# First phase of a two-layer decoder kernel: the cap of the decay inside the masked product, context by feature, cross scores of four strips at once, and a new order

## The reference, cut to what matters

```python
# state-space block: 32 heads of 16 channels, state 128
h = exp(A * dt_t)[...] * h + (dt_t * B_t) x_t ;  y_t = C_t . h          # scan over the 128 tokens
y = _rmsnorm(y + Dp * x_heads, norm_w) * silu(z) ;  x = x + y @ out_proj_w.T
# cross attention, 16 heads of 16 features, keys and values from ctx_1024
q = heads(layernorm(x) @ Wq.T + bq); k = heads(ctx @ Wk.T + bk); v = heads(ctx @ Wv.T + bv)
scores = q k / 4 - 10000 * (1 - mask) ; x = x + softmax(scores) @ v
# then the feed-forward of layer 0: shared expert + top 2 of 16 experts
```

## Time and profile before

| | before |
|---|---|
| median of 3 runs | 4044.49 us (4042.93 to 4050.74) |
| profiled execution, its own time | 4028.71 us |
| span in that profile | 4027.1 us |
| phase 1, 2, 3 (about, from the windows) | 0 to 1780, 1780 to 2080, 2080 to 4027 us |
| busy, whole span | PE 93%, PEld 73%, DVE 77%, ACT 69%, POOL 63% |
| mean granted TensorE clock | 0.973 of full speed |

### The profile page before, as it was taken

How to read it: one execution, slowest core, us unless ns; L and a number is a source line. 1 busy time by engine, 2 the same in 40 slices (tenths; PEclk the granted TensorE clock), 3 DMA queues, 4 the chain that set the end, 5 groups by cost and what they waited for, 6 DMA issues and landing times.

```text
span 4027.1 us, 119475 instructions
## 1 busy us (share of the span) xinstructions
PE 3741.4 (93%) x34582; PEld 2920.7 (73%) x34583; DVE 3082.5 (77%) x8792; ACT 2793.7 (69%) x8434; POOL 2523.8 (63%) x3252
## 2 busy tenths in 40 slices
PE   5999999999999999979978999999999999999997
PEld 4888888888888888867755666666666666666664
DVE  5888888888888888845546777777777777777775
ACT  4778777778888788844436666767667666766764
POOL 4566655656666566622236777777777777777774
PEclk8999999999999999979989999999999999999998
DMA  4334432333333333324420111111011111111110
GB/s 132 134 116 125 137 123 95 115 116 100 111 117 117 116 108 108 113 74 146 144 90 26 34 32 31 34 31 34 28 33 32 32 33 31 34 30 31 32 30 17
DMA packets 222650, 304.24 MB, mean 76 GB/s; under 512 B 57216, under 2 KB 176256, under 8 KB 222592
## 3 DMA queue, kind: packets, MB, share of 16 engines
q1 hardware_dynamic: 197632, 249.83, 19.5%
q0 software_dynamic: 19200, 52.45, 4.0%
q10 hardware_dynamic: 5760, 1.24, 0.2%
HBM read 239.18 MB, written 64.23 MB: 75 GB/s over the span
## 4 chain that ended last, share of the span: by engine, by line
PE 39%; issue 21%; DVE 16%; POOL 10%; ACT 9%; DVEq 2%; DMA 1%; ACTq 1%; POOLq 0%; SPq 0%
PE Q L1553 10%; PE Q L1546 8%; PE Q L1558 5%; PE Q L1933 3%; PE Q L1779 3%; PE Q L1587 3%; POOL arena L673 2%; DVE mx L1135 2%; PE Q L1791 2%; ACT arena L1348 2%; POOL arena L681 1%; ACT arena L1345 1%; PE Q L1874 1%; POOL arena L678 1%; ACT arena L1342 1%
## 5 line engine op out<-in xcount | busy, mean ns | idle before, releaser
L1558 PE MATMUL Q<-ident,arena 128*128 128x128 f32 x3488 | 587.5, 285 | 109.8 <-ACT arena L1282 34.3
L1558 PEld LDWEIGHTS Q<-ident,arena 128*128 128x128 f32 x3488 | 408.3, 143 | 350.0 <-issue 168.3
L1553 PE MATMUL Q<-Wkvl,arena 128*128 128x512 f32 x1024 | 520.8, 601 | 1.5 <-ACT arena L1497 0.8
L673 POOL TENSOR_TENSOR arena<-arena 128x1024 f32<-128x1024 f32 x256 | 481.6, 1902 | 37.0 <-DMA arena<-cum_rows 36.7
L744 POOL TENSOR_TENSOR l<-l,half_pow 128x8 f32<-128x8 f32 x192 | 317.5, 1654 | 146.0 <-DVE l L1154 145.9
L1466 ACT ACTIVATE arena<-Q,mx 128x128 f32<-128x128 f32 x1024 | 359.8, 386 | 6.2 <-DVE mx L1135 6.2
L1381 ACT ACTIVATE arena<-Q,mx 128x128 f32<-128x128 f32 x1024 | 287.2, 386 | 101.5 <-DVE mx L960 97.3
L1546 PE MATMUL Q<-arena,Win 128*128 128x128 f32 x2560 | 347.6, 280 | 1.3 <-DVE arena L890 1.3
L1587 PE MATMUL Q<-ident,arena 128*128 128x128 f32 x2048 | 322.9, 282 | 22.2 <-ACT arena L1381 12.1
L1546 PEld LDWEIGHTS Q<-arena,Win 128*128 128x128 f32 x2560 | 324.9, 196 | 6.3 <-DVE arena L890 2.0
L914 DVE TENSOR_TENSOR arena<-arena,Q 128x1024 f32<-128x1024 f32 x256 | 311.8, 1218 | 14.0 <-ACT arena L1336 7.0
(11 more groups left out here) (292 smaller groups left out, 10195.7 us busy)
## 6 DMA issues: line engine op xcount, KB each, us to landing
arena<-cum_rows SPq DMA_DIRECT2D x256, 512.0 KB, 6.3
arena<-routed_rows SPq DMA_DIRECT2D x144, 128.0 KB, 2.0
expert_rows<-arena POOLq DMA_DIRECT2D x144, 128.0 KB, 2.0
arena<-in_x_dram SPq DMA_DIRECT2D x128, 128.0 KB, 4.4
arena<-in_ctx_dram SPq DMA_DIRECT2D x128, 128.0 KB, 3.0
x_rows<-arena SPq DMA_DIRECT2D x128, 128.0 KB, 1.7
arena<-x_rows SPq DMA_DIRECT2D x128, 128.0 KB, 2.1
out_dram<-arena SPq DMA_DIRECT2D x64, 128.0 KB, 1.7
```

Source lines behind the costliest of these rows:

```text
L673: tell(g.tensor_tensor(E8[j], E8[j], cums[:, 8 * j:8 * j + 8].unsqueeze(2).broadcast_to([P, 8, T]), ALU.subtract), "diff")
L1553: last = mm(out, lhs(c), rhs(c), start=c == 0, stop=c == n - 1)
L1558: last = nc.tensor.transpose(out[:, c * P:(c + 1) * P], src[:, c * P:(c + 1) * P], ident[:, :])
```

## The change

- N: the wide loads take two halves of the partitions: partitions 0 to 63 get all of cum, partitions 64 to 127 get the later 64 tokens twice. `cum_rows` gets a second copy for that (two stores per batch instead of one), and each tile is loaded by two DMAs of 256 KB instead of one of 512 KB. The cap of tile 0 and the absolute values of tiles 1 to 3 are gone: all four tiles get a plain exponential, and the masked product takes min(E, 1) in the same instruction (`scalar_tensor_tensor` in place of `tensor_tensor`).
- O: the square of y2 goes from GpSimd to ScalarE.
- Y: the context is passed in a second time, transposed by the host's layout step, and loaded by feature; the transposes on TensorE and the copy on ScalarE are gone.
- W: the queries are written by ScalarE, in four instructions of 128 x 128, from a bias that is multiplied by `par` once at the start.
- X: all four strips run at once, two groups of heads at a time (`pair(0)`, `pair(1)`), into banks Q5, Q6, Q2 and half of Q4. Maxima and exponentials go in five parts (`PARTS`) of 2, 4, 4, 4 and 2 heads. New waits: `Xs0` for `v0c` and for `cbm` of two batches on, `Nm0` for `P0` (5) of two batches before, `Yk` for `P0` (4).
- A new order of phase 1 on all five engines.

```diff
 ORDER 1:
 SP
-            Ncb0 Yc Ncb1 Mx Ncb2 Ncb3 Gm Ox Xm Dco Go
+            Ncb0 Yc Ncb1 Mx Ncb2 Ncb3 Xm Gm Go Dco Ox
 POOL
-            Nd0 Mln1 Nd1 Nd2 Nd3 Wln2 Gsc Fln3 Osq Oyg Wx1r Orms
+            Nd0 Nd1 Mln1 Nd2 Nd3 Wln2 Gsc Fln3 Oyg Wx1r Orms
 DVE
-            Mln1 Gtop Mln1v Nc0 Wln2 Wln2v Gwt Gslot Gsn Nm0 Zgz Ghg Ddt Nm1 Dsp Ghh Dsr Yk Dss Dsz Ds7 Ds6 Ds5 Nm2 Ds4 Gxo Ds3 Pho Ds2 Phm Ds1 Ds0
-            Phx Dsd Fln3 Dsa Nm3 Fln3v Wq Vcv1 Oy Xm0 Xm1 Vcv2 Oss Fr Vcv3 Fri Bcb Frs Vxs2 Xm2 Xm3 Ox1 Vxdt
+            Gtop Mln1 Gwt Mln1v Gslot Gsn Nm0 Nm1 Zgz Ghg Ghh Yk Wln2 Ddt Wln2v Nm2 Gxo Dsp Dsr Dss Dsz Ds7 Ds6 Nm3 Ds5 Ds4 Ds3 Pho Ds2 Phm Ds1 Ds0
+            Phx Dsd Fln3 Dsa Fln3v Bcb Vcv1 Vcv2 Oy Xm0 Vcv3 Oss Fr Fri Frs Vxs2 Xm1 Xm2 Vxdt Xm3 Ox1 Xm4
 ACT
-            Pt0 Ne0 Mln1 YcT Pt1 Ztz Ne1 Gth Mln1n Nf1 Dab Pt2 Dae Ne2 Pt3 Nf2 Wln2 POT Yv Ne3 Wln2n Nf3 Vcv Dcum Xmr Fln3 Fln3n Xm0 Bbc Xm1 Vcth Frx
-            Xm2 Xm3
+            Ne0 Ztz Ne1 Pt0 Mln1 Gth Pt1 Mln1n Ne2 Pt2 Pt3 Dab Dae Ne3 Wln2 Yv POT Xmr Wln2n Vcv Bbc Wq Dcum Fln3 Fln3n Osq Xm0 Vcth Frx Xm1 Xm2 Xm3
+            Xm4
 PE
-            YcT Pt0 Zz Pt1 Zzh Ggu Gguh Pt2 Mln1n Yk Ddt Pt3 Yv Vip1 Ppv Ppv0 Ppv2 Gdn POT Wln2n Vip1h Wq Dcum Nv0 Nv1 Nv2 Nv3 Xs0 Fln3n Bbc
-            Fr Oss BCB Opr Xs2 Oprh VxsT Frk
+            Zz Zzh Pt0 Yk Ggu Pt1 Gguh Yv Mln1n Pt2 Pt3 Ddt Gdn Ppv Ppv0 Ppv2 Vip1 Vip1h Wln2n POT Bbc Wq BCB Dcum Nv0 Nv1 Nv2 Nv3 Fln3n Xs0 Fr Oss
+            Xs2 Opr VxsT Oprh Frk
 SP, D and N
-                tell(sp.dma_start(rows(cum_d, b), cumT[0:NH, :]), "cum_out", 16)
+                kept, late = (cum_d[bass.ds(b, 1), k, :, :].rearrange("a h t -> (a h) t") for k in range(2))
+                tell(sp.dma_start(kept, cumT[0:NH, :]), "cum_out", 16)
+                tell(sp.dma_start(late.rearrange("h (k t) -> h k t", k=2), cumT[0:NH, HALF:T].unsqueeze(1).broadcast_to([NH, 2, HALF])), "cum_out", 16)
-                    heads8 = cum_d[bass.ds(b, 1), 8 * j:8 * j + 8, :].rearrange("a h t -> (a h t)")
-                    tell(sp.dma_start(Ew[j], heads8.partition_broadcast(P)), f"wide{j}", 16)
+                    for k in range(2):
+                        heads8 = cum_d[bass.ds(b, 1), k, 8 * j:8 * j + 8, :].rearrange("a h t -> (a h t)")
+                        tell(sp.dma_start(Ew[j][k * HALF:(k + 1) * HALF, :], heads8.partition_broadcast(HALF)), f"wide{j}", 16)
 POOL, O: removed
-                tell(g.tensor_tensor(sq0, y2, y2, ALU.mult), "sq")
 DVE, N
-                        tell(v.tensor_scalar(Ew[j], Ew[j], 0.0, None, ALU.min), "cap")
+                    if j == 0 and (not isinstance(b, int) or b >= 2):
+                        done(dve, "P0", b + (-2), 5)
-                    tell(v.tensor_tensor(E8[j], E8[j], Q[4][:, 3 * T:4 * T].unsqueeze(1).broadcast_to([P, 8, T]), ALU.mult), "M")
+                    tell(v.scalar_tensor_tensor(E8[j], E8[j], 1.0, Q[4][:, 3 * T:4 * T].unsqueeze(1).broadcast_to([P, 8, T]), ALU.min, ALU.mult), "M")
 ACT, N, O and W (the two instructions on DVE that wrote QT0 are removed)
-                tell(s_.activation(Ew[1], Ew[1], ACT.Abs), "gap")
-                tell(s_.activation(Ew[1], Ew[1], ACT.Exp, scale=-1.0), "E")
+                for j in range(4):
+                    yield f"e{j}"
+                    done(act, "diff", b, j + 1)
+                    tell(s_.activation(Ew[j], Ew[j], ACT.Exp), "E")
+                tell(s_.activation(sq0, y2, ACT.Square), "sq")
+                for k in range(2):
+                    for c in range(DC):
+                        last = s_.activation(dst[:, c, k, :], src[:, c, :], ACT.Identity, bias=bq0s[:, c, k:k + 1], scale=par[:, k:k + 1])
 PE, Y and X
-                tell(transposes(Q[2], ctx0, DC), "ctxTps")
+                place = lambda j, h: Q[4][:, 0:2 * T] if j == 3 else Q[(5, 6, 2)[j]][:, 2 * h * T:2 * (h + 1) * T]
+                def pair(h):
+                    for j in range(4):
+                        r = slice(32 * j, 32 * j + 32)
+                        mm(place(j, h).rearrange("p (g k) -> p g k", g=2), mask_w[r, :], mrow[r, :].unsqueeze(1).broadcast_to([32, 2, T]), start=True, stop=False)
+                    for g in range(2):
+                        for j in range(4):
+                            r = slice(32 * j, 32 * j + 32)
+                            last = mm(place(j, h)[:, g * T:(g + 1) * T], QT0[r, 2 * h + g, :], KT0[r, h, :], start=False, stop=g == 1)
+                            if g == 1:
+                                tell(last, "S0")
```

More of the change, by code:

```diff
@@ L501, in Y @@
                 yield "c"
-                was(sp, "ctxTps", b)
-                tell(sp.dma_start(ctx0, rows(ctx_d, b)), "ctx0_in", 16)
+                was(sp, "v0", b)
+                tell(sp.dma_start(ctxT, ctxT_d[bass.ds(b, 1)].rearrange("a (c p) t -> p (a c) t", p=P)), "ctx0_in", 16)
             def X(b):
@@ L944, in W @@
                 yield from moments("ln2", x1, stX, mvX, "W_DVE", b)
-                yield "q"
-                done(dve, "q0", b)
-                was(dve, "S0", b, 4)
-                src = cut(Q[2][:, D:2 * D], DC)
-                dst = QT0.rearrange("p (c k) q -> p c k q", k=2)
-                for c in range(DC):
-                    last = v.scalar_tensor_tensor(dst[:, c, :, :], src[:, c, :].unsqueeze(1).broadcast_to([P, 2, T]), bqk0[:, 0, c:c + 1],
-                                                  par[:, :].unsqueeze(2).broadcast_to([P, 2, T]), ALU.add, ALU.mult)
-                tell(last, "q0c")
-            def X(b):
-                banks = (Q[5], Q[6], Q[5], Q[6])
-                for j in range(4):
-                    yield f"m{j}"
-                    done(dve, "S0", b, j + 1)
-                    tell(v.tensor_reduce(mx0[:, 4 * j:4 * j + 4], banks[j][:, :].rearrange("p (g k) -> p g k", g=NG), AX.X, ALU.max, negate=True), "S0max")
+            def X(b):
+                for n, (bank, h, heads) in enumerate(PARTS):
+                    yield f"m{n}"
+                    done(dve, "S0", b, n + 4)
+                    tell(v.tensor_reduce(mx0[:, h:h + heads], Q[bank][:, 0:heads * T].rearrange("p (g k) -> p g k", g=heads), AX.X, ALU.max, negate=True), "S0max")
             def P_(b):
@@ L1369, in W @@
                 copyT("ln2", Q[2], xT2, b)
+                yield "q"
+                done(act, "q0", b)
+                was(act, "S0", b, 8)
+                src = cut(Q[2][:, D:2 * D], DC)
+                dst = QT0.rearrange("p (c k) q -> p c k q", k=2)
+                for k in range(2):
+                    for c in range(DC):
+                        last = s_.activation(dst[:, c, k, :], src[:, c, :], ACT.Identity, bias=bq0s[:, c, k:k + 1], scale=par[:, k:k + 1])
+                tell(last, "q0c")
             def X(b):
-                banks = (Q[5], Q[6], Q[5], Q[6])
                 yield "mr"
                 done(act, "mask0_in", b, 16)
-                was(act, "S0", b, 4)
+                was(act, "S0", b, 8)
                 tell(s_.activation(mrow[:, :], mask0i[:, :], ACT.Identity, bias=eps[:, 2:3]), "mrow")
-                for j in range(4):
-                    yield f"m{j}"
-                    done(act, "S0max", b, j + 1)
-                    for g in range(NG):
-                        last = s_.activation(S0[:, j, g, :], banks[j][:, g * T:(g + 1) * T], ACT.Exp, bias=mx0[:, 4 * j + g:4 * j + g + 1])
+                for n, (bank, first, heads) in enumerate(PARTS):
+                    yield f"m{n}"
+                    done(act, "S0max", b, n + 1)
+                    for h in range(first, first + heads):
+                        last = s_.activation(S0[:, h // 4, h % 4, :], Q[bank][:, (h - first) * T:(h - first + 1) * T], ACT.Exp, bias=mx0[:, h:h + 1])
                     tell(last, "P0")
@@ L1708, in X @@
                 done(pe, "k0c", b)
+                done(pe, "v0c", b)
                 done(pe, "mrow", b)
-                strips(b, banks, (0, 1), QT0, KT0, 0, mask)
+                if not isinstance(b, int) or b + 2 < NB:
+                    done(pe, "cbm", b + 2)
+                pair(0)
                 yield "s2"
-                done(pe, "P0", b, 2)
-                strips(b, banks, (2, 3), QT0, KT0, 0, mask)
+                done(pe, "P0", b, 1)
+                pair(1)
             def P_(b):
@@ L1719, in P_ @@
                     if j < 2:
[L1720 removed]
+                        done(pe, "P0", b, j + 4)
                     else:
```

96 lines of the change are left out of this document (39 added, 57 removed).

## The result

The change made the kernel slower. The changed kernel takes 4075.11 us (median of 4 runs, 4073.78 to 4082.32), the kernel before 4043.71 in the same comparison: a ratio of 1.0077, 95% interval 1.0062 to 1.0092. The prediction had 3957, range 3900 to 4012, and 0.06 for slower. The profiled execution has a span of 4072.4 us, 45.3 more than before.

What follows compares the result with a forecast made beforehand. TensorE was taken to bound phase 1: 23.7 us of work plus 1.05 of waits makes 24.75 us a body, 1.34 less; over 65 bodies 87 us, so 3941 in the profile's like, 3957 us as median, range 3900 to 4012.

Steps and rivals of the forecast that it cites:

- Work of TensorE 23.7 us a body, waits 1.05, body 24.75: Phase 1, TensorE: work falls from 25.1 to 23.7 us, waits go from 0.98 to 1.05, body 1.34 us shorter.
- list of waits: TensorE's waits in the new order: Oss 0.4, VxsT 0.5, Dcum 0.3 to 0.5, Pt0 0 to 0.3 us.
- The masked product at the same price: VectorE: scalar_tensor_tensor costs no more than tensor_tensor, 1218 ns for 1024 columns; other bound 2.3 us, from L885.
- Rival D: VectorE: masked product takes 2.3 us each, a body 27.1 us, the kernel slower at 4110 us; chance 0.05.
- Rival C: ScalarE: the block of score exponentials runs late and holds TensorE; 3990 to 4022 us, chance 0.18.
- DMAs, "I cost it at nothing": SP's queue: five more DMAs in phase 1 delay the first subtraction by about 1.2 us, covered, so priced at nothing.
- a cover of 10.5 us: Phase 1: 8.5 us of TensorE's body behind Dcum plus some 2 us until the first exponential, against a 9.1 us path.
- the new order: Phase 1: the step on which compute waits the reordering makes on TensorE, 1.2 to 1.7 us in place of 0.98.
- Rivals: Better packing 3902 us (0.18), score evacuation limits 4006 (0.18), slow masked product 4110 (0.05), nothing much 4031 (0.06).
- DMA ends the wait of `Nd0`: Sign of being wrong: GpSimd's first subtraction held by its wide load; a lost cover was priced at 1.2 us a body.
- The cuts on the other three engines are worth nothing by themselves; they only loosen waits: Phase 1: less work on VectorE, ScalarE and GpSimd gives no gain by itself, since TensorE stays the bound.
- The doubling that the prediction allowed for: Second store of cum, 256 B runs: if its landing doubled, the path grows by less than 2 us, still covered.

Runs made afterwards that it cites:

- whole_loads: Changed kernel with one store of cum and four wide loads of 512 KB, exponential of a quarter of the difference (not the reference's decay): 3960 us, ratio 0.9808 to before.
- min_only: Kernel before without cap and absolute values, plain exponentials of a quarter of the difference, min(E, 1) in the masked product, whole loads, old order: 4003 us, ratio 0.9864.
- whole_all: whole_loads with the load of x first in SP's order and VectorE's Mln1 and Mln1v moved behind Gsn: 3969 us, ratio 0.9769 to before.
- halves1: whole_loads, still with one store of cum, but each wide load cut into two of 64 partitions, both from the first copy: ratio 0.9880 to before.
- before_split: Kernel before with only the split of the loads: two stores of cum and eight wide loads of 256 KB, compute and order as before: 4100 us, ratio 1.0172.
- slot_first: Changed kernel with VectorE's Mln1 and Mln1v moved behind Gwt, Gslot and Gsn: 4005 us, ratio 0.9917 to before.
- joint: Changed kernel with its two stores of cum, but each tile's two halves loaded by one DMA of 512 KB: 6011 us, ratio 1.479 to before.
- joint_all: joint with the load of x first in SP's order and VectorE's Mln1 and Mln1v behind Gwt, Gslot and Gsn: 6024 us, ratio 1.482 to before.

## Why the prediction was wrong

- *Work of TensorE 23.7 us a body, waits 1.05, body 24.75*: right, for a kernel with whole loads (24.83), and in part by luck. Scores and masks 1.34 us, estimated 1.26. The waits stood where they were put: 0.4 at `VxsT` (1.37 from 1053.43, work 0.97; predicted 0.5), 0.4 at `Dcum`, and 0.2 at `Oss` where 0.4 was expected. whole_loads has the same three, 1.0 together, which leaves 23.8 of work. But the prediction's own list of waits added to 1.2 to 1.7, and it took 1.05; and of the 26.09 before it had counted 0.98 as waits and missed the 0.2 before `Ggu`. So the work fell by 1.1, not 1.36, and the waits fell by 0.2 where a rise of 0.07 was put; the two errors nearly cancel.
- *The masked product at the same price*: right, 1220 ns against 1218. Rival D did not happen. But its bound was a misreading (last section). Rival C did not happen either: the 14 exponentials end where tile 0's exponential starts, at 1058.89, and `Pt0` on TensorE waits 0.1 us at most (1.97 us from 1056.67 to 1058.64, 1.89 for the same x16 elsewhere).
- *DMAs, "I cost it at nothing"*: this is the step that failed. It followed one transfer, tile 0, to one consumer, `Nd0`, and compared it with a cover of 10.5 us. The sizes were off: the step took the second store and the second half to make it 1.2 us later; from the store to the start of the subtraction it is 7.8 us now (1048.69 to 1056.46), 6.0 before, 1.8 more, and GpSimd waited 2.8 us for it. For tile 0 the cover just held all the same: the subtraction ended at 1058.36, 9.7 us behind the store, and ScalarE came to the first exponential at 1058.89, 10.2 behind it; it was tile 1's exponential that waited, 0.8 us. What failed is that it left out what stands behind in SP's line: `Mx`. The additional store takes 0.5 us there, each additional half 0.7, x went from 3.5 to 6.2 us behind the store, and its load lands in 4.9 us. VectorE waits 1.9 us a body for it and TensorE 1.6 for the slots behind (rows above), where the step had priced a lost cover at 1.2. The prediction named SP's queue and counted five more DMAs, but asked only when the moved DMAs arrive, not what they are put in front of.
- *"the new order"*: it put `Mln1` ahead of `Gwt` and `Gslot` on VectorE, and `Ggu` soon after the start of TensorE's body. The prediction went through the waits that the new order makes between compute engines, not the one for a load.
- *Rivals*: none of them was this. "DMA ends the wait of `Nd0`" stood among the signs of being wrong, with a price of 1.2 us a body and no chance of its own.
- *"The cuts on the other three engines are worth nothing by themselves; they only loosen waits"*: the second half was right and made the first wrong. min_only is 1.4% faster, 0.54 us a body at full clock and 0.73 in the mean, from ScalarE's and VectorE's work alone. With whole loads, strips, context, queries, square and order together add 0.6 to 1.0% more (whole_loads and whole_all against min_only); none of these was run by itself.
- *Arithmetic of the loss*: without the split the changed kernel is at 0.981, with it at 1.008; of the expected gain of 87 us 81 were there (4041 - 3960), most of it (1.4% of the 1.9) the part that min_only has and the prediction had put at nothing, and 109 us (2.7% of 4040) were lost again to the loads.

## What to carry to other kernels

When a change adds DMAs to a queue that issues in order, list what stands behind them in that queue, and who waits for each of these: here the victim was the load of x, not the loads that were split. When every engine gets less busy and the time goes up, stop looking at engines and follow the chain of waits across a body until it closes. Cutting a broadcast load into two of 64 partitions wasn't free here, and two costs on one covered path took more together than one by one.

## What the runs showed of the hardware

- *Half the partitions, more engine time.* The same 2 MB a batch in 64-partition DMAs of 256 KB instead of 128-partition ones of 512 KB take the DMA engines 25.1% of 4016 us (halves1) instead of 19.7% of 3956 (whole_loads), 1008 us against 779, at nearly as many packets (209920 and 205824). A half of 256 KB takes 5.2 us to land there (median, 1000 to 1400 us) where a whole of 512 KB takes 6.0. The first subtraction starts 5.1 us after the first issue in the changed kernel, 4.1 us in whole_loads (medians, 600 to 1400 us). Why halves are dear is open.
- *A store in runs of 256 B.* With the second store, a store of cum takes 1.7 us to land in place of 1.4 (medians, 1000 to 1400 us, both stores together); the second one of the body shown took 1.9. SP waits for both: 2.7 us from the first store to the first load (1048.69 to 1051.37), 1.7 in whole_loads. Half of the difference is the second issue, 0.5 us behind the first, half that it lands later. The doubling that the prediction allowed for did not show.
- *VectorE held by GpSimd.* The silu product, with two inputs in SBUF, took 1146 ns in the mean before and 681 in the changed kernel, the same instruction. Before, it started at 1035.63 while GpSimd's subtraction ran from 1034.21 to 1036.10: 0.47 of waiting and 0.55 more to its end at 1036.65. In before_split it takes 691 to 2437 ns, and which it is depends on who starts first. Of 30 from 600 to 1400 us, the six that start up to 0.1 us after a subtraction take 2.35 to 2.42 us and end 0.54 or 0.55 after it; all that start ahead of the subtraction, or beside none, take 0.69. And Gwt, two elements a partition, went from 229 to 1024 ns in the changed kernel:

```profile
1060.16 1.12 DVE L1042 TENSOR_SCALAR meta<-rt 128x2 f32<-128x2 f32 x1
```

```profile
1059.37 1.90 POOL L682 TENSOR_TENSOR arena<-arena 128x1024 f32<-128x1024 f32 x1 [1.01 <-DMA arena<-cum_rows]
```

  It ends as GpSimd's instruction does (1061.28 and 1061.27), and so do all 30 from 600 to 1400 us, within 0.03 us. In slot_first, where about half of them meet no subtraction, the median is 230 ns. So these two forms of VectorE are held until a GpSimd subtraction that was there first has ended. The masked product, with one input in PSUM, isn't: 1211 to 1223 ns in all 256, some of them beside a subtraction (two from 1061.87 take 2.35 us, the subtraction starts at 1062.70). The busy time of such a row is partly a wait, and no row of the waits shows it.
- *Clock.* The granted clock in phase 1 was 0.98 before, 1.00 in min_only, and 0.96 to 0.97 in every kernel with the new order (300 to 1700 us) but joint and joint_all, which are at 0.71 and 0.70 with TensorE busy for 791 and 820 of 1400 us. TensorE's busy time in the others was less than before: 1289 us of 1400 in the changed kernel, 1345 in whole_loads, 1360 before, 1351 in min_only. The lower clock is part of the difference between 24.83 us at full clock and 25.21 in the mean of the loop of whole_loads; how large a part was not worked out. What of the new order does it was not tried. It does not make the changed kernel slower than before, since whole_loads has it too and is 1.9% faster.
